# Keys and queries with channels on the partitions, ordered by half, pair and head, and a new order of all steps

## What is computed

```
Q = (query @ Wq.T + bq).reshape(b, sq, H, D).transpose(0, 2, 1, 3)   # H = 16 heads, D = 16
K = (key @ Wk.T + bk).reshape(b, sk, H, D).transpose(0, 2, 1, 3)
V = (value @ Wv.T + bv).reshape(b, sk, H, D).transpose(0, 2, 1, 3)
# apply_rope: x2 = stack([-x[..., 1::2], x[..., 0::2]], -1).reshape(x.shape); x*cos + x2*sin
Q, K = apply_rope(Q, cos_q, sin_q), apply_rope(K, cos_k, sin_k)
scores = einsum('bhqd,bhkd->bhqk', Q, K) * SCALE      # then mask, softmax, times V, @ Wo.T + bo
```

## Time and profile before

| what | us |
|---|---|
| median of 3 runs | 956.42 (955.5 to 958.2) |
| the profiled execution, its own time | 957.39 |
| its span | 955.6 |
| TensorE busy | 832.9 (87%) |
| VectorE busy | 689.7 (72%) |
| ScalarE busy | 544.1 (57%) |
| GpSimd busy | 300.1 (31%) |

### The profile page before, as it was taken

The page is one execution under the profiler, slowest core; times in us unless marked ns, Lnnn a source line. Parts: engine busy times, 40 slices in busy tenths (PEclk is TensorE's granted clock), DMA queues, the critical chain, the costliest instruction groups (busy, mean ns, idle before and its releaser), DMA issues.

```text
span 955.6 us, 17622 instructions
## 1 busy us (share of the span) xinstructions
PE 832.9 (87%) x6750; PEld 629.4 (66%) x6750; DVE 689.7 (72%) x1249; ACT 544.1 (57%) x909; POOL 300.1 (31%) x483
## 2 busy tenths in 40 slices
PE   1557789999999999999989999999999999997876
PEld 1233457786777777686867677676867677775655
DVE  8566578686969787786869696886869697866332
ACT  2453756657484747657574747566574747472331
POOL 5331415142423315151433334051424334141001
PEclk9876799999999999999999999999999999999999
DMA  8033160707052441707061532607070524325000
GB/s 277 0 59 53 45 79 16 108 13 117 8 101 34 71 64 41 94 13 122 14 106 17 90 46 52 83 27 108 14 114 10 101 34 62 62 38 75 1 12 22
DMA packets 98323, 57.43 MB, mean 60 GB/s; under 512 B 7841, under 2 KB 97473, under 8 KB 98241
## 3 DMA queue, kind: packets, MB, share of 16 engines
q1 hardware_dynamic: 98240, 56.31, 35.7%
HBM read 39.24 MB, written 16.79 MB: 59 GB/s over the span
## 4 chain that ended last, share of the span: by engine, by line
PE 47%; DVE 22%; DMA 10%; ACT 9%; issue 7%; POOL 2%; SPq 2%; DVEq 0%; ACTq 0%; POOLq 0%
PE bankC L1006 12%; PE bankA L816 11%; PE bankC L991 6%; DMA out<-x 6%; PE bankA L942 5%; PE slotB L910 3%; PE slotB L929 3%; PE bankA L807 3%; DMA q_st<-m_lo 3%; DVE x L1234 3%; DVE bn L1226 2%; DVE st L1204 2%; DVE nmax L1283 2%; ACT L666 2%; POOL rstd L534 2%
## 5 line engine op out<-in xcount | busy, mean ns | idle before, releaser
L1006 PE MATMUL bankC<-h0h,w 128*128 128x256 f16 x1024 | 233.4, 273 | 6.7 <-DVE h0l L1327 6.7
L1006 PE MATMUL bankC<-h0l,w 128*128 128x256 f16 x1024 | 232.9, 273 | 0.0
L1283 DVE TENSOR_REDUCE nmax<-slotB 128x4 f32<-128x1024 f32 x128 | 153.2, 1218 | 7.5 <-PE slotB L910 6.7
L716 ACT ACTIVATE pr<-slotB 128x1024 f32<-128x1024 f32 x128 | 129.3, 1025 | 37.6 <-PE slotB L929 37.4
L1006 PEld LDWEIGHTS bankC<-h0h,w 128*128 128x128 f16 x1024 | 100.5, 98 | 22.7 <-issue 9.8
L1006 PEld LDWEIGHTS bankC<-h0l,w 128*128 128x128 f16 x1024 | 100.4, 98 | 11.9
L533 POOL TENSOR_SCALAR rstd<-mv 128x2 f32<-128x2 f32 x48 | 9.3, 193 | 295.6 <-DVE mv L1229 295.6
L910 PE MATMUL slotB<-k_st,q_st 97*128 97x256 bf16 x512 | 78.9, 279 | 8.1 <-issue 5.1
L929 PE MATMUL slotB<-q_st,k_st 99*128 99x256 bf16 x512 | 75.9, 276 | 8.4 <-DMA q_st<-m_lo 4.8
L498 POOL TENSOR_SCALAR st<-st 128x2 f32<-128x2 f32 x32 | 7.7, 240 | 230.9 <-ACT junk L658 194.1
L1327 DVE SCALAR_TENSOR_TENSOR h1l<-bankC,h1h 128x512 f16<-128x512 f32 x64 | 43.6, 682 | 41.9 <-ACT h1h L741 41.9
(11 more groups left out here) (197 smaller groups left out, 1789.5 us busy)
## 6 DMA issues: line engine op xcount, KB each, us to landing
k_st<-scr SPq DMA_DIRECT2D x96, 128.0 KB, 5.2
q_st<-scr SPq DMA_DIRECT2D x96, 128.0 KB, 4.9
scr<-kpart SPq DMA_DIRECT2D x16, 384.0 KB, 3.6
scr<-qpart SPq DMA_DIRECT2D x16, 384.0 KB, 3.7
x<-in_x SPq DMA_DIRECT2D x16, 256.0 KB, 2.9
cT<-in_ctxT SPq DMA_DIRECT2D x16, 256.0 KB, 2.9
out<-x SPq DMA_DIRECT2D x16, 256.0 KB, 5.3
pr<-in_k SPq DMA_DIRECT2D x1, 1024.0 KB, 10.2
```

Source lines behind the costliest of these rows:

```text
L716: act.activation(pr[i % 2][:, c, :, :].rearrange("p h s -> p (h s)"), slotB[ringB.slot(g, name)][:, :], ACT.Exp, scale=DH ** -0.5).then_in ...
L1006: ins = pe.matmul(bankC[ringC.slot(g, name)][:, e * T:(e + 1) * T], w_1[:, i // 2, (2 * m + e) * P:(2 * m + e + 1) * P], (h0h, h0l)[i % 2] ...
L1283: dve.tensor_reduce(nmax[:, hg * HG * NT + n:(hg + 1) * HG * NT:NT], slotB[ringB.slot(g, name)][:, :].rearrange("p (h s) -> p h s", s=S), ...
```

## The change

Keys and queries come out of TensorE with channels on the partitions. The weights' columns are put in order of (half e, pair i, head h), where the head channel is 2i+e, so that the rotation of a channel and its partner are the two halves of one tile, at the same partition. The step `kT` (four pairs of matmuls, 256 columns wide) and the step `v` take the place of `kv0` and `kv1`; the bias becomes a column, added as ScalarE (keys) or VectorE (queries) empties the bank; the tables of cosine and sine are spread and transposed once, at the start (`w:rope`, `w:bqk`, `w:wk`, `w:wq`). `rotk` has three groups of operations instead of four. `krT` and `qrT` are gone from TensorE, ScalarE's and VectorE's splitting (`kp`, `qp`) now reads SBUF. In `scr` the channel is `(d h)`, each partition of `k_st` or `q_st` gets one run of 8 KB. The whole table `TIMES` and `BEGIN` have new numbers.

```diff
@@ TIMES, BEGIN @@
-    kv0 P36.62 A40.7 | kv1 P41.76 A45.67 | rotk G52.07 | krT P63.53 A62.23 V69.67 G65.68 | kput S56.02 | kget S61.88
+    kT P41.81 A55.22 | v P42.7 A66.7 | rotk G78.52 | kp A71.59 V74.64 G94 | kput S76.9 | kget S87.55
...
@@ SyncE @@
-                                 scr[g % 2, n, i].rearrange("(h d) t -> d h t", d=DH)).then_inc(arrived.sem, 16)
+                                 scr[g % 2, n, i].rearrange("(d h) t -> d h t", d=DH)).then_inc(arrived.sem, 16)
@@ GpSimd @@
             def rotk(g):
-                pool.wait_ge(*ringA.emptied(g, "kv0"))
-                pool.wait_ge(*ringA.emptied(g, "kv1"))
-                k, t1, t2 = heads(kb), heads(kt1), heads(kt2)
-                pool.tensor_tensor(t1, k, cos_all, ALU.mult)
+                pool.wait_ge(*ringA.emptied(g, "kT"))
...
+                pool.tensor_tensor(kt1[:, :, :], kb[:, :, :], cosT, ALU.mult)
                 for e in range(2):
-                    ins = pool.tensor_tensor(t2[:, :, :, e::2], k[:, :, :, 1 - e::2], sin_all[e], ALU.mult)
+                    ins = pool.tensor_tensor(kt2[:, e, :], kb[:, 1 - e, :], sinT[:, e, :], ALU.mult)
                 own.settle(ins)
-                own.settle(pool.tensor_tensor(kt1[:, :, :], kt1[:, :, :], kt2[:, :, :], ALU.add))
-                pool.tensor_tensor(kt1[:, :, :], kt1[:, :, :], rbk[:, :, :], ALU.add).then_inc(kt_s.sem, 1)
+                pool.tensor_tensor(kt1[:, :, :], kt1[:, :, :], kt2[:, :, :], ALU.add).then_inc(kt_s.sem, 1)
@@ ScalarE @@
+            def keys(g):
...
+                act.wait_ge(*ringA.filled(g, "kT"))
+                for e in range(2):
+                    ins = act.activation(kb[:, e, :], bankA[ringA.slot(g, "kT")][:, e * T:(e + 1) * T], ACT.Identity,
+                                         bias=bcol[:, e:e + 1])
+                ins.then_inc(ringA.free_sem(g, "kT"), 1)
...
+            def first_part(g, turned, t, part, gone, done):
                 if g >= 1:
                     act.wait_ge(*gone.at(g - 1))
-                act.wait_ge(*ringA.filled(g, name))
+                act.wait_ge(*turned.at(g))
+                act.activation(part[:, 0], t[:, :, :], ACT.Copy).then_inc(done.sem, 1)
@@ TensorE @@
-            def krT_(g):
-                pe.wait_ge(*kt_s.at(g))
-                transposed(g, "krT", kt1)
+            def across_channels(g, name, w, xT):
+                take(g, ringA, name)
+                for e in range(2):
+                    for c in range(CT):
+                        ins = pe.matmul(bankA[ringA.slot(g, name)][:, e * T:(e + 1) * T], w[:, c, e * P:(e + 1) * P],
+                                        xT[:, c, :], start=c == 0, stop=c == CT - 1)
+                ins.then_inc(ringA.full_sem(g, name), 1)
...
-                projected(g, "q", w_q, (0, D), x1T, [0, 1])
-            def qrT_(g):
-                pe.wait_ge(*qr_s.at(g))
-                transposed(g, "qrT", qt1)
+                across_channels(g, "q", w_q, x1T)
```

More of the change, by code:

```diff
@@ L52 @@
 TIMES = """
[L53 to L57, removed]
@@ L68 @@
[L68 to L72, removed]
@@ L73 @@
[L73 to L74 removed]
+    w:s V-478.88 P-418.9 | w:m V-233.31 A-335.78 P-239.8 | w:a V-140.22 | w:iv V-8.92 | w:g1 V-131.73 P-3.44
+    w:g2 V-12.53 A-10.39 P12.85 | w:gate V35.16 | w:down V39.11 | w:bv P73.77 A78.32 | w:bias P87.08 V99.85
+    w:mask V80.1 S-74.71 | w:sgn V47.89 | w:k0 V71.86 | w:k2 V54.66 | w:k1.0 A51.04 | w:k1.1 A57.97 | w:k1.2 A87.6
@@ new lines @@
+    w:k1.3 A116.07 | w:rope G22.67 P24.43 A0.45 | w:bqk P39 A49.94 | w:wk G37.27 | w:wq G43.01 | loadx S76.36
+    loadc S85.33 | scale A0 G20.62 V21.31 | stat1 G31.46 | round V28.63 | xqT P33.45 A34.05
+    iv0 P38.19 A41.31 V43.73 | iv1 P39.93 A46.92 V43.24 | a P35.51 A35.66 | aT P37.8 A38.45 | sq A47.64
+    ivT P41.32 V48.52 | cum V49.57 | recur V50.51 | rec P52.46 A57.82 V51.67 | max2 V51.75 | stat2 G72.59
+    round2 V52.48 | rqT P64.32 A63.11 | gate0 P65.22 A67.73 V57.36 | gate1 P66.62 A70.4 V58.32 | stat3 G80.11
@@ new lines @@
+    max P123.14 A126.41 V113.54 | maxrow S125.38 | exp0.0 P126.52 A128.77 | exp0.1 P127.1 A129.6 | pv0 P130.22
+    exp1.0 P128.98 A129.71 | exp1.1 P129.4 A132.2 | pv1 P131.69 A133.71 | exp2.0 P130.47 A132.27
+    exp2.1 P131.23 A133.28 | pv2 P135.49 | exp3.0 P132.11 A133.85 | exp3.1 P132.48 A138.09 | pv3 P138.93 A140.49
+    oTok P141.9 V143.37 | oT P144.48 A143.61 | wo P145.37 V144.91 | bn2 V148.17 G179.2 | x2 V154.13
+    x2T P148.46 A159.82 V156.33 | l0_0 P149.49 A160.12 V157.13 | l0_1 P150.73 A163.44 V157.83
@@ L103 @@
            "gate0": ("ACT", "gate0"), "gate1": ("ACT", "gate1"), "sqT0": ("ACT", "sqT0"), "sqT1": ("ACT", "sqT1"),
-           "down": ("DVE", "down"), "kv0": ("ACT", "kv0"), "kv1": ("ACT", "kv1"), "x1T": ("ACT", "x1T"),
-           "q": ("DVE", "q"), "krT": ("DVE", "krT"), "qrT": ("DVE", "qrT"),
+           "down": ("DVE", "down"), "kT": ("ACT", "kT"), "v": ("ACT", "v"), "x1T": ("ACT", "x1T"), "q": ("DVE", "q"),
            "pv0": ("ACT", "pv1"), "pv2": ("ACT", "pv3")}
@@ L1033, in _ @@
                      "gate1": lambda g: gate_(g, 1), "sqT0": lambda g: sqT_(g, 0), "sqT1": lambda g: sqT_(g, 1),
-                     "down": down_, "kv0": lambda g: kv_(g, 0), "kv1": lambda g: kv_(g, 1), "krT": krT_, "x1T": x1T_,
-                     "q": q_, "qrT": qrT_, "max": max_, "oTok": oTok_, "oT": oT_, "wo": wo_, "x2T": x2T_}
+                     "down": down_, "w:rope": angles, "w:bqk": qk_bias, "kT": kT_, "v": v_, "x1T": x1T_,
+                     "q": q_, "max": max_, "oTok": oTok_, "oT": oT_, "wo": wo_, "x2T": x2T_}
             for un in range(NT * NHG):
@@ L1345, in _ @@
                      "gate1": lambda g: gate_largest(g, 1), "round3": round3, "down": down_, "bn": moments1, "x1": x1_,
-                     "krT": k_parts, "q": q_, "rotq": rotq, "qrT": q_parts, "max": max_low, "oTok": divided,
+                     "kp": k_parts, "q": q_, "rotq": rotq, "qp": q_parts, "max": max_low, "oTok": divided,
                      "wo": residual2, "bn2": moments2, "x2": x2_, "x2T": x2_low, "l2.3": last_layer, "bn3": moments3}
```

189 lines of the change are left out of this document (118 added, 71 removed).

## The result

The changed kernel took 923.0 us in the median of 4 runs (921.25 to 924.43), the kernel before 957.31 beside it: 0.963 of the time, interval 0.957 to 0.968. The profiled execution took 922.5 us, its span is 920.3. The prediction was 929 (908 to 954), faster.

A forecast was written before the change was run, and what follows sets the result against it. TensorE was taken to carry the period, busy 95% of 52.94 us. Fourteen periods at 51.2 save 24.4 us, the ends 3: 957.4 - 27.4 = 930.0, one less for the median, 929 us (908 to 954).

The forecast's parts named there:

- The walk: One undisturbed period, `exp0.0` to `exp0.0` in three legs: 50.7 us; with 0.5 added for joins 51.2, against 52.94.
- Transposes: On TensorE, dropping the eight of `krT` and `qrT` saves 0.88 us a period, 14.1 in 16 batches.
- The norm and `xb`: VectorE's pair at `x1` falls from 2.59 to about 0.8 us, `x1T` stops waiting: 0.8 us a period gained.
- round2: VectorE's pair waits out GpSimd's `xb` at its new place, ends 0.95 us later, TensorE waits at `rqT`: 0.95 paid.
- the rival without the hold: `xb` does not hold `round2` on VectorE: 14 x 0.95 = 13 us less, 916 (905 to 920); chance 0.10.
- The store: Lands in 3 us, `wo` then waits for TensorE only; worth 1.1 us against the long-store period, nearly nothing against the other.
- The rival of a slow store: 8 KB runs no quicker than 512-byte rows: store lands after 5 us, `wo` waits, period up to 1.1 longer, 944.
- The chain of `m_lo`: From `rqT` through `scale`, `rotk`, `kp`, `m_hi`, `m_lo` to `exp0.0`: 9.6 us against TensorE's 9.3, 0.3 of wait.
- Joins and ends: 0.5 us a period added for joins the walk misses; first batch gains 2 us, last batch 1, together 3.
- Only the transposes: Stalls close one wait and open the next, only TensorE's removed transposes count: 942 (938 to 950); chance 0.24.
- No net change: The maximum's chain, `iv1` and TensorE's order keep the period at 52.9: 954 to 959; chance 0.10.
- slower: Keys' rotation on GpSimd gates the exponentials: 4 us more gives period 55, 985 us; 2.5 more gives 962; chance 0.11.

The follow-up runs named there:

- the aligned pieces: Changed kernel with scratch rows 1024 bytes apart, so reads are again 512-byte pieces, each starting at a multiple of 512 bytes: 947.0 us, ratio 0.986.

## Why the prediction was right, point by point

*The walk.* In the quiet period of the trace after, `exp0.0` stands at 510.12, `oTok` at 524.14, the first `l1` at 543.6, the next `exp0.0` at 560.29. The legs are 14.02, 19.5 and 16.7, forecast at 14.05, 19.3 and 17.35: together 50.2 for 50.7. In the chain of 508 to 562, and in the row of the `l1` matmuls (first and last start after the durations):

```profile
510.12 0.44 PE slotB L990 x4
...
524.14 1.06 PE slotB L1014 x8
...
548.63 1.03 DVE st L1260
...
560.29 0.44 PE slotB L990 x4
```

```profile
L1067 PE MATMUL bankC<-h0h,w x56: 269/273/275, 543.6 to 561.2; 128*128 128x256 f16 x56
```

The first two legs were right to 0.2. The third was forecast 0.65 too long, with `round2`'s hold in both. What it saved besides isn't settled; TensorE's busy time fell by 1.2 a period, to 48.9 where the prediction looked for 49.2, so up to 0.3 of it can be work.

*Transposes.* Forecast 14.1 us; eight put back cost 9.8. The term was too large by 4.3, since part of the work falls into waits.

*The norm and `xb`.* `x1`'s pair went to 0.73 for a forecast of 0.8, the wait at `x1T` is gone, and the forecast 0.8 a period (11.2 us in 14) is close to what the kernel before gained by moving `xb` alone, 0.71 a period and 11.1 us in all. The reading behind it was a little too narrow: the pair at `x1` was the held one in eight periods of fourteen, `round1`'s in the other six.

*round2.* The mechanism and the place were right, and so was the size of undoing it: 14 x 0.95 = 13 us were forecast for the rival without the hold, and 11.6 were measured with `xb` moved. But that move also shortened GpSimd's row by 1.27, and the hold itself is 0.87 in twelve periods of fourteen. The instruction was another one too: not the rounding pair but the 128x2 operation just ahead of it took the whole hold. The Trainium skill, "SBUF — State Buffer", section "Who interferes with whom", which the prediction cited for the two-port modes, has this case as well: it says that a VectorE instruction with two SBUF inputs contends with a GpSimd instruction that reads SBUF. The trace agrees: L1260, with two inputs of 128x2, took 1.02 for 0.16 us and ended with `xb`.

*The store.* This is the term that was mis-sized. The prediction took a landing at 3 us and `wo` waiting for TensorE only, with the worth of the long runs at up to 1.1 us a period. The store lands at 4.1, `wo` still waits 1.0 a period for it, yet long runs are worth 1.6 a period in the new order, 24 us in all: the bounds were drawn from two periods of the kernel before, where VectorE waited 1.18 a period for the store, and in the new order with pieces it waits 2.26. The rival of a slow store gave 944, and the aligned pieces gave 947.0.

*The chain of `m_lo`.* 9.6 against 9.3 was right to within what can be told: longer by 1.27 the chain costs 1.12 a period, and without its longest link it gains nothing. It is the last condition in two periods of the changed kernel, not in each. But the prediction saw `m_lo`'s new place as a mere condition of this chain. The experiment shows it as worth 18.5 us in the new order and nothing in the old.

*Rotation.* `rotk` 4.0 for 4.1, `rotq`'s sine parts 0.98 for 1.10 each.

*Joins and ends.* The quiet period has no 0.5 for joins: the walk's 50.7 was already 0.5 more than its 50.2. The mean is 50.83 mainly because other periods wait for the store, which the walk had left out. Of the twelve periods from 201.96 to 812.64, VectorE waits over 1.2 us for it in six, and five of these take 51.1 to 51.7; of the six others five take 50.0 to 50.4. So the period's forecast of 51.2 came within 0.4 partly by luck, two terms too large against one left out. The ends gained 4.9 for 3. From 27.4 forecast it is 6.0 more in the periods (14 x 0.43) and 1.9 more at the ends, less 0.4 outside the span: 34.9, which is 957.4 less 922.5.

*The signs.* Of those named ahead, `x1`'s pair, the missing wait at `x1T`, `rotk` and the period came as said. Wrong were the store's landing, `wo`'s wait, `round2`'s pair at 1.6 (it took 0.61, with the hold ahead of it) and the 0.9 at `rqT`: its row shows 0.39.

*The rivals.* Only the transposes (942): falls by the wait at `x1T` and by what four edits cost. No net change and slower: not seen. The slow one's mechanism is real, and the rotation 1.27 us longer met it at once. Its two prices don't come out of one sum: from a period of 55 at 985 us, 1.5 less a period is 21 less, 964 and not 962.

The parts don't add up to the gain. Undone one by one they cost 24 (runs of 8 KB), 18.5 (`m_lo`) and 9.8 (transposes), 52 together, against 34 gained, even before `x1`; `xb` alone was worth 11 in the old order. Each price holds only in the order in which it was measured.

## What to carry to other kernels

Walk one undisturbed period leg by leg with net prices from the chain; it came within 0.5 us of 50 here. Then look at the periods that are not quiet: the store's wait was in those. When a long GpSimd operation is moved, look at what VectorE does at the new place, down to its smallest operation: here the better place was where GpSimd otherwise waits for VectorE, and a single number of the table was worth 11 us in either kernel. Before a transfer is made quicker for its own sake, see who waits for the transfers queued behind it: the reads landed 0.5 us sooner than in pieces, and most of the 24 us between the two kernels shows at the store.

## What the hardware showed that was not expected

A run of 8 KB per partition against 16 pieces of 512 bytes changed the landing of a 128 KB read little, 4.6 us for 5.1, but the store behind it by 1.2. Rows 528 bytes apart, with the same number of packets (98512 on the queue in both), cost 16 us more than rows 1024 bytes apart (962.8 and 947.0), and made this kernel as slow as the one before the change. A VectorE operation on 128x2 values took 1.02 us instead of 0.16 when it came just behind the start of a GpSimd operation of 1.27 us; with that operation moved away, it took 0.15.
